# First differences taken by GpSimd between two normalizations' small steps, and the last tile's copy and difference in two halves

## The chip, the cores and the metric

The kernel runs on one core of one Trainium2 chip. The metric is the device time of one execution in microseconds (us). A core has TensorE (PE in the profile; its weight loads are listed as PEld), VectorE (DVE), ScalarE (ACT) and GpSimd (POOL), each with an instruction queue of its own that is worked off in order, and SyncE (SP), which issues the DMAs here. The engines are kept in step by semaphores: an instruction can wait for a semaphore to reach a value and can raise one when it is done.

## The reference

A Flamingo-style block over x of shape 4 x 2048 x 512, all in float32:

```python
x = x + tanh(g_xattn) * xattn(layernorm(x), ctx)      # 16 heads of 32, 154 context tokens, Wq Wk Wv Wo
x = x + tanh(g_ffn) * ffn(layernorm(x))

def ffn(x):                                           # x_prev: the token before, zero for the first
    xr = mu_r * x + (1 - mu_r) * x_prev
    xk = mu_k * x + (1 - mu_k) * x_prev
    r = sigmoid(xr @ W_r.T)
    k = xk @ W_k.T
    return r * (square(relu(k)) @ W_v.T)
```

Since mu * x + (1 - mu) * x_prev is mu * (x - x_prev) + x_prev, the kernel needs the difference of each token and the one before it. That difference is what the change is about.

## The kernel before

The 8192 tokens are worked in 16 blocks of N = 512 tokens; a block is TT = 4 tiles of 128 tokens, and the 512 channels are C = 4 chunks of 128. Each engine has a function step(i, ffn, pre), written out by hand: step 0 and step 15 stand alone and steps 1 to 14 are the body of a loop. The order of the instructions in each engine's step is the order of the work; nothing else schedules it. In step i the attention of block i, the feed-forward part of block i - 1 and the queries of block i + 1 are interleaved.

Matmuls in float32 are done as three products of a rounded high part and a low part. So a value that goes into a product is first mixed or copied (into a PSUM bank or a buffer), then ScalarE writes the high part (line 543), and VectorE or GpSimd subtracts it to get the low part (line 780 on VectorE, 463, 471 and 475 on GpSimd).

The stretch around the change is the second layernorm and the token mix. For block i, tile t:

- VectorE, residual (lines 879 to 884): x1 = projection + x (line 882), then the moments: bn_stats (811), the negated mean nm (814), bn_aggr (816).
- GpSimd, norm(1, i, t) (lines 434 to 445): three small operations on 128 x 1 values: variance plus epsilon (439), its power -1/2, rstd (441), and the bias nb (445). For t = 3 the third is left out.
- The normalized tile xn2: ScalarE for t = 0, 1, 2 (norm2, line 597), VectorE for t = 3 (norm2_last, line 890: a subtract and a multiply with one value per partition, SBUF to SBUF, 128 x 512).
- TensorE, x2_transposed (lines 1202 to 1211): four 128 x 128 transposes (line 1073) into o_bank or d_bank.
- ScalarE, x2_copy (lines 654 to 658): the bank is copied to x2, chunks by channels, tokens along the free dimension.
- The first difference diff = x2 - x2 shifted by one token, from SBUF to SBUF, 128 x 512 for a tile: GpSimd for t = 0, 1, 2 (difference, lines 452 to 459), VectorE for t = 3 (difference_last, lines 893 to 897). In the profile diff has the name place, since it lies in that tensor.
- VectorE, mix_k (lines 904 to 909): xk = diff * mu_k + x2 for a whole chunk (all 512 tokens), into o_bank or d_bank; both tensor inputs lie in SBUF. ScalarE then writes the high part of xk (xk_high), VectorE the low part (xk_low), and TensorE's ffn_k of the next step waits for xk_low chunk by chunk (line 1222).

GpSimd's order in this stretch is norm 0, norm 1, difference 0, norm 2, norm 3, difference 1, difference 2 (lines 518 to 524), and then it waits until all four chunks are mixed (line 526). VectorE's is residual 0 to 3 with maxima between, norm2_last, difference_last, mix_k 0 and 1, xk_low 0, gated (line 877, the feed-forward product of the block before), xk_low 1, mix_k 2 and 3, xk_low 2 and 3 (lines 1016 to 1036). TensorE's is the last projection, x2_transposed 1, query 3 of the next block with x2_transposed 2 before its last chunk, x2_transposed 3, ffn_v of tile 3 of the block before, maxima 4, and then the next step's ffn_k (lines 1353 to 1361).

Of the kernel before, what the change touches and what calls it, by code (L numbers as in the profile page):

```python
# [8 lines left out]
ALU = mybir.AluOpType  # L9
ACT = mybir.ActivationFunctionType  # L10
# [7 lines left out]
def flamingo_block(nc, x, ctx_columns, g_xattn, g_ffn, Wq, Wk, Wv, Wo, W_r, W_k, W_v, mu_r, mu_k, out):  # L18
# [8 lines left out]
    P = 128  # L27
    C = D // P
    G = H // 4
    N = 512  # L30
    TT = N // P
# [17 lines left out]
    with ExitStack() as ctx:  # L49
# [6 lines left out]
        def sem(name):  # L56
            return ctx.enter_context(nc.semaphore(name))
# [58 lines left out]
        diff = place[:, 4:8, :]  # L116
# [48 lines left out]
        x2_done, x2_ready = sem("x2_done"), sem("x2_ready")  # L165
        x2_first, carry_ready = sem("x2_first"), sem("carry_ready")
        diff_ready = sem("diff_ready")
        xn2_last, diff_last = sem("xn2_last"), sem("diff_last")
        xk_mixed, xk_hi = sem("xk_mixed"), sem("xk_hi")
        xr_mixed, xr_hi = sem("xr_mixed"), sem("xr_hi")  # L170
        xk_lo, xr_lo = sem("xk_lo"), sem("xr_lo")
# [12 lines left out]
        x2_bank = [(o_bank, d_bank)[t % 2] for t in range(TT)]  # L184
# [209 lines left out]
        def _(pool):  # L394
# [39 lines left out]
            def norm(which, i, t):  # L434

                n = i * TT + t + 1
                last = which == 1 and t == TT - 1
                pool.wait_ge(mean_ready[which], 2 * n)
                nc.gpsimd.tensor_tensor(ve[:, which, t:t + 1], mv[:, which, t, 1:2], eps[:, :], ALU.add).then_inc(var_eps_ready[which], 1)  # L439
                pool.wait_ge(var_eps_ready[which], n)  # L440
                nc.gpsimd.tensor_tensor(rstd[:, which, t:t + 1], ve[:, which, t:t + 1], minus_half[:, :], ALU.pow).then_inc(rstd_ready[which], 1)
                if last:
                    return
                pool.wait_ge(rstd_ready[which], n)
                nc.gpsimd.tensor_tensor(nb[:, which, t:t + 1], nm[:, which, t:t + 1], rstd[:, which, t:t + 1], ALU.mult).then_inc(norm_ready[which], 1)  # L445
# [6 lines left out]
            def difference(i, t):  # L452

                pool.wait_ge(x2_ready, i * TT + t + 1)
                if t == 0:
                    pool.wait_ge(x2_first, i + 1)
                    pool.wait_ge(attn_hi, (i + 1) * G)
                tokens, before = slice(1 + P * t, 1 + P * t + P), slice(P * t, P * t + P)
                nc.gpsimd.tensor_tensor(diff[:, :, before], x2[:, :, tokens], x2[:, :, before], ALU.subtract).then_inc(diff_ready, 1)
# [35 lines left out]
            def step(i, ffn, pre):  # L495
                if ffn:
                    k2_parts(i - 1)
                if pre:
                    norm(0, i + 1, 0)
                    norm(0, i + 1, 1)  # L500
                for g in range(1, G):
                    attn_low(i, g - 1)
                    if ffn:
                        output(i - 1, g - 1)
                    if pre:
                        for t in ((2, 3), (), ())[g - 1]:
                            norm(0, i + 1, t)
                attn_low(i, G - 1)
                if pre:
                    for g in range(G - 1):  # L510
                        q_low(i + 1, g)
                if not ffn:

                    pool.wait_ge(kv_done, KV_UNITS)
                    for n in range(7):
                        pool.wait_ge(later_stored[n], LATER_STORES[n])
                first_column(i)
                norm(1, i, 0)
                norm(1, i, 1)
                difference(i, 0)  # L520
                norm(1, i, 2)
                norm(1, i, 3)
                for t in range(1, TT - 1):
                    difference(i, t)

                pool.wait_ge(xk_mixed, (i + 1) * C)
                if pre:
                    q_low(i + 1, 3)
                if ffn:
                    output(i - 1, TT - 1)  # L530
# [10 lines left out]
        def _(act):  # L541
# [112 lines left out]
            def x2_copy(i, t):  # L654
                act.wait_ge(x2_done, i * TT + t + 1)
                later(act, r_done, i * TT)
                nc.scalar.activation(x2[:, :, 1 + P * t:1 + P * t + P],
                                     x2_bank[t][:, :].rearrange("p (c n) -> p c n", c=C), ACT.Copy).then_inc(x2_ready, 1)

            def mix_high(i, dst, c, src, mixed_ready, hi_ready):  # L660
                act.wait_ge(mixed_ready, i * C + c + 1)
# [116 lines left out]
        def _(dve):  # L778
# [111 lines left out]
                nc.vector.tensor_scalar(xn2[t % 2], x1[:, t, :], mv[:, 1, t, 0:1], rstd[:, 1, t:t + 1],  # L890
                                        ALU.subtract, ALU.mult).then_inc(xn2_last, 1)

            def difference_last(i):
                dve.wait_ge(diff_ready, (i + 1) * (TT - 1))
                dve.wait_ge(x2_ready, (i + 1) * TT)
                nc.vector.tensor_tensor(diff[:, :, N - P:N], x2[:, :, N - P + 1:N + 1], x2[:, :, N - P:N],
                                        ALU.subtract).then_inc(diff_last, 1)

            def keep_carry(i):
                dve.wait_ge(x2_ready, (i + 1) * TT)  # L900
# [1 line left out]
                nc.vector.tensor_copy(carry[:, :], x2[:, :, N]).then_inc(carry_ready, 1)  # L902

            def mix_k(i, c):
                if c == 0:
                    dve.wait_ge(diff_last, i + 1)
                elif c >= 2:
                    dve.wait_ge(xk_lo, i * C + c - 1)
                nc.vector.scalar_tensor_tensor(xk_bank[c][:, :], diff[:, c, :], mu[:, 1, c:c + 1], x2[:, c, 0:N], ALU.mult, ALU.add).then_inc(xk_mixed, 1)  # L909

# [42 lines left out]
            def step(i, ffn, pre):  # L953
                reduce_max(i, 4)
                if ffn:
                    mix_r(i - 1, 0)
                else:
                    kv_low_part(G + 1)
                reduce_max(i, 5)
                if not ffn:  # L960
                    ctx_low(1)
                if ffn:
                    xr_low(i - 1, 0)
                    mix_r(i - 1, 1)
                    mix_r(i - 1, 2)
                    xr_low(i - 1, 1)
                    mix_r(i - 1, 3)
                    xr_low(i - 1, 2)
                    k_relu(i - 1, 2)
                p_low(i, 0, 0)  # L970
                if ffn:
                    xr_low(i - 1, 3)
                p_low(i, 0, 1)
                p_low(i, 0, 2)
                p_low(i, 0, 3)
                if not ffn:
                    kv_low_part(FIRST_LATER)
                p_low(i, 0, 4)
                if ffn:
                    k_relu(i - 1, 3)  # L980
                if not ffn:
                    fill_group(0)
                if pre:
                    moments1(i + 1, 0)
                    moments1(i + 1, 1)
                for g in range(1, G):
                    attend(i, g - 1)
                    p_low(i, g, 0)
                    p_low(i, g, 1)
                    if ffn and g == 2:  # L990
                        gated(i - 1, 1, V_BANK[1])
                    if not ffn and g == 3:
                        kv_low_part(KV_UNITS - 1)
                    if pre and g == 3:
                        xT_low(i + 1, 0)
                    p_low(i, g, 2)
                    p_low(i, g, 3)
                    if not ffn and g < 3:
                        kv_low_part(FIRST_LATER + 2 * g)
                    p_low(i, g, 4)  # L1000
                    if ffn and g != 2:
                        gated(i - 1, g - 1, V_BANK[g - 1])
                    if not ffn and g < 3:
                        fill_group(g)
                    if pre and g == 1:
                        moments1(i + 1, 2)
                        moments1(i + 1, 3)
                if pre:
                    for t in range(1, TT):
                        xT_low(i + 1, t)  # L1010
                attend(i, G - 1)
                if pre:
                    reduce_max(i + 1, 0)
                    reduce_max(i + 1, 1)
                    reduce_max(i + 1, 2)
                residual(i, 0, pre)
                if pre:
                    reduce_max(i + 1, 3, (0, 1))
                residual(i, 1, pre)
                if pre:  # L1020
                    reduce_max(i + 1, 3, (2, 3))
                residual(i, 2, pre)
                residual(i, 3, pre)
                norm2_last(i)
                difference_last(i)
                mix_k(i, 0)
                mix_k(i, 1)
                xk_low(i, 0)
                if ffn:
                    gated(i - 1, TT - 1, V_BANK[TT - 1] if pre else V3_END)  # L1030
                xk_low(i, 1)
                mix_k(i, 2)
                mix_k(i, 3)
                xk_low(i, 2)
                xk_low(i, 3)
                keep_carry(i)
# [380 lines left out]
```

## Time and profile before

| | us |
|---|---|
| median of 3 runs | 1425.04 |
| the 3 runs | 1425.04, 1425.04, 1422.91 |
| the profiled execution: its time | 1423.38 |
| the profiled execution: its span | 1421.7 |
| PE busy in the span | 1355.7 (95%) |
| DVE busy | 1054.9 (74%) |
| ACT busy | 776.1 (55%) |
| POOL busy | 577.2 (41%) |
| mean granted TensorE clock | 0.989 of full speed |

The busy shares are of the span. A share of 95% for TensorE says that the time is its own work plus its pauses; a pause is what another engine can take away or add. The other engines are idle much of the time, so their work costs something only where TensorE, or the chain that TensorE waits for, has to wait for it.

### The profile page before, as it was taken

To read this page: it belongs to the slowest core of one execution; us is meant where nothing else is said; L and a number is where in the kernel's file an instruction comes from. 1 tells how busy PE (TensorE), PEld (TensorE's weight loads), DVE (VectorE), ACT (ScalarE), POOL (GpSimd) and SP (SyncE) were. 2 spreads that over 40 slices of the span, in tenths; PEclk is the share of its full clock that TensorE was granted. 3 is DMA by queue.
4 is the path that set the end of the run, shared out by engine and by line. 5 is a ranking of instruction groups with operands and counts; after the bars stand their busy time and mean duration, and the time that the engine had idled before them with its cause. 6 is when DMAs were issued, how large, how long until landed. Compare 5 with 4: busy or idle time off the path is not lost.

```text
span 1421.7 us, 27928 instructions
## 1 busy us (share of the span) xinstructions
PE 1355.7 (95%) x9436; PEld 990.4 (70%) x9436; DVE 1054.9 (74%) x1924; ACT 776.1 (55%) x1424; POOL 577.2 (41%) x774
## 2 busy tenths in 40 slices
PE   4989999999999999999999999999999999999988
PEld 3656676776767777676777767677776767777657
DVE  4887778687787868778686877868677786877652
ACT  3583746557374654737466473645637465563632
POOL 2113435344353534435253443525335352534333
PEclk7999999999999999999999999999999999999989
DMA  6631111211012121111212111121201112120101
GB/s 190 219 87 44 40 45 52 73 52 52 22 66 59 52 73 52 47 27 59 66 52 73 38 48 39 59 66 52 66 25 63 44 59 66 52 65 17 45 15 45
DMA packets 98795, 84.07 MB, mean 59 GB/s; under 512 B 49488, under 2 KB 63824, under 8 KB 98768
## 3 DMA queue, kind: packets, MB, share of 16 engines
q1 hardware_dynamic: 98768, 83.72, 19.5%
q8 instruction: 15, 0.25, 0.1%
q14 instruction: 12, 0.10, 0.0%
HBM read 58.79 MB, written 20.71 MB: 56 GB/s over the span
## 4 chain that ended last, share of the span: by engine, by line
PE 75%; DVE 13%; ACT 8%; issue 3%; POOL 1%; DMA 0%; ACTq 0%; DVEq 0%
PE g_bank L1067 41%; PE g_bank L1227 7%; PE o_bank L1174 6%; PE s_bank L1148 4%; PE d_bank L1180 4%; ACT s_bank L638 3%; ACT pq L637 3%; PE s_bank L1124 3%; PE s_bank L1158 2%; DVE buf L780 2%; DVE o_bank L909 2%; ACT buf L543 1%; DVE xa L890 1%; DVE d_bank L909 1%; PE s_bank L1067 1%
## 5 line engine op out<-in xcount | busy, mean ns | idle before, releaser
L850 DVE TENSOR_TENSOR pq<-s_bank,pq 128x512 f16<-128x512 f32 x320 | 220.2, 689 | 69.4 <-ACT s_bank L638 69.1
L846 DVE TENSOR_REDUCE mm<-s_bank 128x3 f32<-128x462 f32 (+1 forms) x384 | 198.8, 577 | 92.9 <-PE s_bank L1124 92.7
L637 ACT ACTIVATE pq<-s_bank 128x512 f16<-128x512 f32 x320 | 192.1, 600 | 86.6 <-PE s_bank L1152 86.6
L1227 PE MATMUL g_bank<-buf,WkT 128*128 128x512 f32 x744 | 196.6, 411 | 12.8 <-DVE buf L780 12.7
L1067 PE MATMUL g_bank<-xnT,WqT 128*128 128x512 f32 x768 | 199.2, 405 | 4.4 <-DVE xnT L834 4.4
L638 ACT ACTIVATE s_bank<-s_bank 128x512 f32<-128x512 f32 x320 | 194.6, 608 | 0.0
L1067 PE MATMUL g_bank<-WoT,buf 128*128 128x512 f32 x768 | 193.3, 401 | 0.0
L1067 PE MATMUL g_bank<-WrT,buf 128*128 128x512 f32 x744 | 184.2, 396 | 0.0
L475 POOL TENSOR_TENSOR buf<-place,buf 128x512 fp32r<-128x512 f32 x64 | 82.6, 1291 | 235.4 <-ACT buf L543 235.4
L1227 PEld LDWEIGHTS g_bank<-buf,WkT 128*128 128x128 f32 x744 | 136.6, 192 | 55.9 <-DVE buf L780 17.5
L1067 PE MATMUL g_bank<-WvT,buf 128*128 128x512 f32 x708 | 174.2, 395 | 0.0
L1067 PEld LDWEIGHTS g_bank<-xnT,WqT 128*128 128x128 f32 x768 | 139.7, 190 | 40.5 <-DVE xnT L834 5.9
L1067 PEld LDWEIGHTS g_bank<-WrT,buf 128*128 128x128 f32 x744 | 137.8, 188 | 40.2 <-issue 11.3
L1067 PEld LDWEIGHTS g_bank<-WoT,buf 128*128 128x128 f32 x768 | 140.7, 188 | 32.7
L1067 PEld LDWEIGHTS g_bank<-WvT,buf 128*128 128x128 f32 x708 | 130.6, 188 | 32.5 <-issue 5.8
L463 POOL TENSOR_TENSOR buf<-xa,buf 128x512 fp32r<-128x512 f32 x64 | 82.2, 1284 | 168.9 <-DVE d_bank L909 89.5
L543 ACT ACTIVATE buf<-place 128x512 fp32r<-128x512 f32 x128 | 81.0, 633 | 106.3 <-DVE place L867 71.7
L471 POOL TENSOR_TENSOR buf<-place,buf 128x512 fp32r<-128x512 f32 x64 | 83.3, 1301 | 93.9 <-ACT buf L543 93.9
L483 POOL TENSOR_TENSOR x<-place,x 128x512 f32<-128x512 f32 x48 | 61.7, 1285 | 123.1 <-DVE place L877 123.1
L597 ACT ACTIVATE xa<-x,nb,rstd 128x512 f32<-128x512 f32 x48 | 39.0, 812 | 105.3 <-POOL nb L445 104.9
L439 POOL TENSOR_TENSOR ve<-mv,eps 128x1 f32<-128x1 f32 x128 | 24.3, 190 | 164.2 <-DVE mv L816 164.2
L467 POOL TENSOR_TENSOR place<-place 128x512 f32<-128x512 f32 x64 | 78.0, 1218 | 25.5 <-ACT place L629 25.5
(140 smaller groups left out, 2096.4 us busy)
## 6 DMA issues: line engine op xcount, KB each, us to landing
xa<-in_x SPq DMA_DIRECT2D x64, 256.0 KB, 3.4
x<-in_x SPq DMA_DIRECT2D x64, 256.0 KB, 2.8
out<-x SPq DMA_DIRECT2D x48, 256.0 KB, 2.0
k_all<-k_scratch SPq DMA_DIRECT2D x16, 256.0 KB, 2.9
k_low<-k_scratch SPq DMA_DIRECT2D x16, 256.0 KB, 3.0
v_main<-v_scratch SPq DMA_DIRECT2D x16, 256.0 KB, 2.8
place<-x SPq DMA_DIRECT2D x16, 256.0 KB, 2.4
out<-place SPq DMA_DIRECT2D x16, 256.0 KB, 2.0
```

The source lines that it names most:

```text
L463: nc.gpsimd.tensor_tensor(buf4[:, LO, g, :], q32[g], buf4[:, HI, g, :].bitcast(F32), ALU.subtract).then_inc(q_lo, 1)
L467: nc.gpsimd.tensor_tensor(k2[c % 2], k2[c % 2], k2[c % 2], ALU.mult).then_inc(k2_ready, 1)
L471: nc.gpsimd.tensor_tensor(buf1[:, LO, c, :], k2[c % 2], buf1[:, HI, c, :].bitcast(F32), ALU.subtract).then_inc(k2_lo, 1)
L475: nc.gpsimd.tensor_tensor(buf3[:, LO, g, :], attn32, buf3[:, HI, g, :].bitcast(F32), ALU.subtract).then_inc(attn_lo, 1)
L543: nc.scalar.activation(dst, src, ACT.Copy).then_inc(done, 1)
L637: nc.scalar.activation(pq[:, n, HI, :], bank[:, :], ACT.Exp, scale=SCALE).then_inc(p_hi, 1)
L638: nc.scalar.activation(bank[:, :], bank[:, :], ACT.Exp, scale=SCALE).then_inc(p_full, 1)
L846: nc.vector.reduce_max(maxima, scores, AX.X).then_inc(reduced, 1)
L850: nc.vector.tensor_tensor(pq[:, n, LO, :], score_bank[5 * g + n][:, :], pq[:, n, HI, :], ALU.subtract).then_inc(p_lo, 1)
L1067: ins = nc.tensor.matmul(dst, stationary(s, c), moving(m, c), start=(c, n) == (0, 0), stop=(c, n) == (chunks - 1, len(PRODUCTS) - 1))
L1174: nc.tensor.matmul(o_bank[rows(j), :], v, pq[:, 4 if n else j, q, :], start=(n, k) == (0, 0), stop=(n, k) == (1, 2))
L1227: ins = nc.tensor.matmul(bank[c][:, :], WkT2[:, s, e, cols(c)], buf3[:, m, e, :], start=(e, n) == (0, 0), stop=(e, n) == (C - 1, len(PRODU ...
```

## The change

Three things are changed.

1. GpSimd's order: difference 1 now stands between norm 2 and norm 3, and difference 2 after norm 3. Nothing is added or taken away on GpSimd.
2. The copy of the last tile (x2_copy with t = 3, ScalarE) is two instructions of two chunks each. The first raises the new semaphore x2_half, the second raises x2_ready.
3. difference_last (VectorE) is two instructions of two chunks each, each with its own semaphore. mix_k 0 stands between them and waits only for the first; mix_k 2 waits for the second.

```diff
@@ gpsimd step
                 difference(i, 0)
                 norm(1, i, 2)
+                difference(i, 1)
                 norm(1, i, 3)
-                for t in range(1, TT - 1):
-                    difference(i, t)
+                difference(i, 2)
@@ scalar
             def x2_copy(i, t):
                 act.wait_ge(x2_done, i * TT + t + 1)
                 later(act, r_done, i * TT)
-                nc.scalar.activation(x2[:, :, 1 + P * t:1 + P * t + P],
-                                     x2_bank[t][:, :].rearrange("p (c n) -> p c n", c=C), ACT.Copy).then_inc(x2_ready, 1)
+                dst, src = x2[:, :, 1 + P * t:1 + P * t + P], x2_bank[t][:, :].rearrange("p (c n) -> p c n", c=C)
+                if t < TT - 1:
+                    nc.scalar.activation(dst, src, ACT.Copy).then_inc(x2_ready, 1)
+                else:
+                    nc.scalar.activation(dst[:, 0:2, :], src[:, 0:2, :], ACT.Copy).then_inc(x2_half, 1)
+                    nc.scalar.activation(dst[:, 2:4, :], src[:, 2:4, :], ACT.Copy).then_inc(x2_ready, 1)
@@ vector
-            def difference_last(i):
-                dve.wait_ge(diff_ready, (i + 1) * (TT - 1))
-                dve.wait_ge(x2_ready, (i + 1) * TT)
-                nc.vector.tensor_tensor(diff[:, :, N - P:N], x2[:, :, N - P + 1:N + 1], x2[:, :, N - P:N],
-                                        ALU.subtract).then_inc(diff_last, 1)
+            def difference_last(i, half):
+                if half == 0:
+                    dve.wait_ge(diff_ready, (i + 1) * (TT - 1))
+                    dve.wait_ge(x2_half, i + 1)
+                else:
+                    dve.wait_ge(x2_ready, (i + 1) * TT)
+                chunks = slice(2 * half, 2 * half + 2)
+                nc.vector.tensor_tensor(diff[:, chunks, N - P:N], x2[:, chunks, N - P + 1:N + 1], x2[:, chunks, N - P:N],
+                                        ALU.subtract).then_inc(diff_last[half], 1)
             def mix_k(i, c):
-                if c == 0:
-                    dve.wait_ge(diff_last, i + 1)
-                elif c >= 2:
+                if c % 2 == 0:
+                    dve.wait_ge(diff_last[c // 2], i + 1)
+                if c >= 2:
                     dve.wait_ge(xk_lo, i * C + c - 1)
@@ vector step
-                difference_last(i)
+                difference_last(i, 0)
                 mix_k(i, 0)
+                difference_last(i, 1)
                 mix_k(i, 1)
```

## Rows read from the trace of the kernel before

**Rows 1.** Windows: one loop body; length, PE busy (instructions), granted clock, DMA, GB/s.

```profile
631.90:715.60 83.70, 82.19 (x583) 1.00 0.17 53
```

**Rows 2.** Timeline of TensorE, steady stretch: start, duration, engine, line, idle before and releaser.

```profile
655.75 0.83 PE L1174 MATMUL o_bank<-pq,v_main 128*32 128x512 f16 x12 [0.49 <-DVE pq L850]
...
715.50 0.95 PE L1067 MATMUL g_bank<-xnT,WqT 128*128 128x512 f32 x3
716.90 0.66 PE L1073 MATMUL d_bank<-ident,xa 128*128 128x128 f32 x4 [0.45 <-DVE xa L890]
...
721.19 3.05 PE L1227 MATMUL g_bank<-buf,WkT 128*128 128x512 f32 x12 [0.40 <-DVE buf L780]
724.41 3.06 PE L1227 MATMUL g_bank<-buf,WkT 128*128 128x512 f32 x12 [0.17 <-DVE buf L780]
```

**Rows 3.** Timeline of VectorE over the same stretch.

```profile
715.59 1.25 DVE L890 TENSOR_SCALAR xa<-x,mv,rstd 128x512 f32<-128x512 f32 x1 [0.94 <-POOL rstd L441]
718.30 0.69 DVE L896 TENSOR_TENSOR place<-x 128x512 f32<-128x512 f32 x1 [1.45 <-ACT x L657]
719.02 0.76 DVE L909 SCALAR_TENSOR_TENSOR o_bank<-place,mu,x 128x512 f32<-128x512 f32 x1
719.69 0.76 DVE L909 SCALAR_TENSOR_TENSOR d_bank<-place,mu,x 128x512 f32<-128x512 f32 x1
720.45 0.69 DVE L780 TENSOR_TENSOR buf<-o_bank,buf 128x512 fp32r<-128x512 f32 x1
```

**Rows 4.** Timeline of GpSimd over the same stretch.

```profile
710.71 1.04 POOL L459 TENSOR_TENSOR place<-x 128x512 f32<-128x512 f32 x1
...
714.73 0.19 POOL L439 TENSOR_TENSOR ve<-mv,eps 128x1 f32<-128x1 f32 x1 [1.39 <-DVE mv L816]
715.00 0.55 POOL L441 TENSOR_TENSOR rstd<-ve,minus_half 128x1 f32<-128x1 f32 x1
715.52 2.22 POOL L459 TENSOR_TENSOR place<-x 128x512 f32<-128x512 f32 x2
```

**Rows 5.** Timeline of ScalarE: the four copies to x2 lie at line 657.

```profile
710.03 0.60 ACT L657 ACTIVATE x<-o_bank 128x512 f32<-128x512 f32 x1 [1.66 <-PE o_bank L1073]
...
713.26 0.60 ACT L657 ACTIVATE x<-d_bank 128x512 f32<-128x512 f32 x1 [1.79 <-PE d_bank L1073]
...
715.78 0.60 ACT L657 ACTIVATE x<-o_bank 128x512 f32<-128x512 f32 x1 [1.22 <-PE o_bank L1073]
717.59 0.60 ACT L657 ACTIVATE x<-d_bank 128x512 f32<-128x512 f32 x1 [1.21 <-PE d_bank L1073]
718.09 0.59 ACT L543 ACTIVATE buf<-g_bank 128x512 fp32r<-128x512 f32 x1
```

**Rows 6.** Lines 890 (all 16), 783, 459 (two here): duration ns min/median/max.

```profile
L890 DVE TENSOR_SCALAR xa<-x,mv,rstd x16: 1254/1254/1255, 128.5 to 1376.4; 128x512 f32<-128x512 f32 x16
...
L783 DVE CAST negsel<-place x1: 427/427/427, 3.2 to 3.2; 128x512 fp32r<-128x512 f32 x1
...
L459 POOL TENSOR_TENSOR place<-x x2: 1040/1131/1222, 715.5 to 716.5; 128x512 f32<-128x512 f32 x2
```

**Rows 7.** Timeline of VectorE and GpSimd where they lie side by side elsewhere.

```profile
740.36 1.04 POOL L467 TENSOR_TENSOR place<-place 128x512 f32<-128x512 f32 x1
...
740.46 0.22 DVE L814 TENSOR_SCALAR nm<-stats 128x1 f32<-128x1 f32 x1
...
1318.12 0.76 DVE L919 SCALAR_TENSOR_TENSOR d_bank<-place,mu,x 128x512 f32<-128x512 f32 x1
...
1318.26 1.51 POOL L467 TENSOR_TENSOR place<-place 128x512 f32<-128x512 f32 x1
```

**Rows 8.** Groups of instructions by shape, first 110 us: halves of 128x256; mean ns last.

```profile
L780 DVE TENSOR_TENSOR buf<-s_bank,buf 128x256 fp32r<-128x256 f32 x4 | 1.7, 424 | 8.7 <-ACT buf L543 8.7
L543 ACT ACTIVATE buf<-s_bank 128x256 fp32r<-128x256 f32 x4 | 1.5, 368 | 2.3 <-PE s_bank L1067 2.3
```

**Rows 9.** Timeline of TensorE in the last step.

```profile
1377.73 0.66 PE L1073 MATMUL d_bank<-ident,xa 128*128 128x128 f32 x4 [0.94 <-DVE xa L890]
```

More of the change, by code:

```diff
@@ L167, in flamingo_block @@
         diff_ready = sem("diff_ready")
-        xn2_last, diff_last = sem("xn2_last"), sem("diff_last")
+        xn2_last, x2_half = sem("xn2_last"), sem("x2_half")
+        diff_last = [sem("diff_last01"), sem("diff_last23")]
         xk_mixed, xk_hi = sem("xk_mixed"), sem("xk_hi")
```

## The prediction

> **What bounds the kernel now.** I read the windows first, to see how far TensorE fills a loop body; then TensorE's timeline for its pauses; then the chain of waits to see what each pause hangs on; then the timelines of the other engines around it. A loop body takes 83.70 us, of which TensorE is busy 82.19 at full clock [rows 1]. The 1.51 us of pause stand at four places [rows 2]: 0.49 before an attention product (here from the body before; it comes back once per body), 0.45 before the last tile's transposes at 716.90, 0.40 before ffn_k at 721.19, and 0.17 before its third chunk at 724.41. The last three hang on one chain, which a reader can follow through the rows: GpSimd's rstd of tile 3 ends at 715.55 [rows 4], norm2_last runs 715.59 to 716.84 [rows 3], the transposes start at 716.90, ScalarE copies them 717.59 to 718.19 [rows 5], then difference_last at 718.30, mix_k 0 at 719.02, mix_k 1 at 719.69, xk_low 0 from 720.45 to 721.14 [rows 3], and TensorE at 721.19. From there VectorE goes on without a break to xk_low 2, for which TensorE waits at 724.41. So a microsecond off this chain is a microsecond per body, as long as TensorE is not the later one.
>
> **Norm2_last, and what stands beside it.** It takes 1254 ns in each of its 16 instances, while the only other one-input 128x512 operation of VectorE from SBUF to SBUF with no partner on GpSimd took 427 [rows 6]. Difference 1 of GpSimd starts at 715.52, 0.07 us before norm2_last, and is the 1040 ns one of the two in that row, so it ends at 716.56; norm2_last ends 0.28 later. Difference 2, queued behind it, takes 1222 in place of 1040 [rows 4, 6]. That is how two instructions look that cannot run together: VectorE's waits for difference 1 to end, and difference 2 then waits for VectorE's. Once VectorE is first with two SBUF inputs, GpSimd's operation lasts 1.51 us instead of 1.04 [rows 7].
>
> The Trainium skill, page "SBUF — State Buffer", section "Who interferes with whom", states this as a rule: a VectorE tensor_scalar in a two-port mode and a GpSimd instruction exclude each other, and the second one blocks until the first is done. By that rule norm2_last costs its free duration once difference 1 is out of its way; without it the 1254 ns would be its own and stay. The trace agrees with the rule, by the 1254, the 427 and the stretched 1222.
>
> **Part 1, GpSimd's order.** Difference 1 now needs x2_copy 1, which ends at 713.86; a copy's end is followed by the difference 0.08 later where GpSimd is free (710.63, then 710.71) [rows 4, 5]. So it runs 713.94 to 714.98. The next GpSimd instruction starts 1.00 after it (the two differences of 1.04 and 1.22 fill 2.22, the second starting at 716.52), at 714.94, where norm 3 started at 714.73: norm 3 is 0.21 late. This is the cost of the move. It is queued on rstd: rstd ends 715.76, norm2_last starts 715.80. VectorE's operations beside difference 1 are residual 3, bn_stats, nm and bn_aggr. Difference 0 lies beside the same of tile 2 and takes 1.04; for the 128x1 operation there is a row of its own, 0.22 us inside a GpSimd operation of 1.04 [rows 7], so I charge nothing. If nm were held till 714.98, it would cost 0.6 in norm 3 (bound, below).
> Norm2_last without a partner: 427 by its nearest row, 280 if only what was left after difference 1 counts, 1254 if it is its own. I take 430: it ends 716.23, 0.61 earlier than 716.84. Difference 2 waits for x2_copy 2 (ends 716.38 [rows 5]) and starts 716.46, after norm2_last, and ends 717.50. TensorE has its last query matmuls from 715.50 for 0.95, the successors in such a queue start about 0.15 before that modelled end, at 716.30; so the transposes start at about 716.29 instead of 716.90. TensorE is just free: its 0.45 pause goes. ScalarE's copy starts 716.98 instead of 717.59; its copy 2 is over by then.
>
> **Parts 2 and 3, the halves.** A half costs ScalarE 368 ns and VectorE 424 [rows 8], against 600 and 692 for the whole, so two halves cost about 140 and 160 ns more. ScalarE: first half 716.98 to 717.35, second from 717.25 (whole ones overlap by 0.10 [rows 5]) to 717.62. The query copies behind them start 0.03 after that minus overlap, still 0.5 earlier than before: hidden. VectorE: by x2_half difference_last could start at 717.46 (0.11 after its release, as 718.19 to 718.30), but it also waits for difference 2, which ends at 717.50; with the second wait behind it I take 717.60. Difference 2 is the new last release here. Then 0.45 to mix_k 0 (718.05), 0.67 to the second half (718.72; 0.67 is the distance of the two mixes [rows 3]), 0.45 to mix_k 1 (719.17), 0.67 to xk_low 0 (719.84), whose high part is long there. Before it was 720.45, since xk_low 0 had to wait for the high part of chunk 0. Gain: 0.61. With one whole difference it would be 717.67, mix_k 0 at 718.39, high part done at 719.78, xk_low 0 at 719.82: the halves give nothing and cost nothing, -0.02 to +0.02. The range for the halves: 0.13 better if difference 2 is not what is waited for, 0.13 worse if a half costs VectorE 0.49 in place of 0.42.
>
> The Trainium skill, "VectorE: DVE Perf Modes", section "The TRN2 errata", speaks against halves: a fixed cost per instruction, which many small tiles pay each. The rows agree (2 x 424 against 692), and that cost is in the sum.
>
> **Behind it.** Gated follows at 720.44; it needs ffn_v 3, which TensorE starts at 716.70 instead of 717.31 and ends at 719.7. ffn_k starts at 720.58 instead of 721.19, its third chunk at 723.80 instead of 724.41, because VectorE's queue from xk_low 0 on has the same instructions at the same distances. The fourth pause (0.49, waiting for attention weights that ScalarE and VectorE made from scores that TensorE made) starts from TensorE's own instructions and shifts with it. GpSimd waits after difference 2 for all four mixes, so nothing is queued there; SyncE's copy of x1 starts on norm2_last, earlier too.
>
> **Sum.** 15 steps (0 to 14) x 0.61 = 9.15. The last step has another TensorE order: the transposes wait 0.94 for norm2_last [rows 9], and ffn_k waits for xk_low 0 alone. With norm2_last at 1376.42 + 0.21 + 0.43 = 1377.06 and difference 2 no longer late, the same steps give 0.7. Together 9.85, or 9.9 us: 1423.4 of the profiled execution becomes 1413.5. The runs shown are 1422.91 to 1425.04 with the median at the upper end, so the median of the changed kernel lies between 1413.0 and 1415.2; I say 1414.5.
>
> **Rivals.**
> - *Nm is held by difference 1.* nm 714.98, rstd ends 716.15, norm2_last 716.19 to 716.62, difference 2 starts after it and ends 717.7, difference_last 717.8: a gain of 0.41 per step, 6.6 us, 1418. For it: nm is a tensor_scalar like norm2_last. Against: the 0.22 us one of [rows 7]. The same time comes out if difference 2 or the halves cost 0.2 more than I take. Chance 0.17.
> - *The later pause takes it back.* If the 0.49 pause hangs on something that does not shift (a load, GpSimd's queue), it grows to up to 1.1 and the gain is near 0: 1422 to 1426. For it: nothing in the rows but that this is the pause that I follow least. Against: its releaser is VectorE behind ScalarE behind TensorE. Chance 0.08.
> - *Slower: norm2_last is long by itself, and the move only delays it.* Then it starts 0.21 late and still takes 1254. Transposes at 717.11, first half copied at 718.18, difference_last 718.29, xk_low 0 at 720.53: 0.08 per step, 1.3 us, which is no change. It gets slower from the point where difference 1 in front of norm 3 takes 1222 rather than 1040: 0.39 late, 0.26 per step, 4.2 us, 1429. For it: 1254 never varies. Against: the 427 and the 280 left. Chance 0.05.
> - Otherwise my forecast, 0.55 to 0.75 per step, 1411.5 to 1416.5 with the spread of runs: 0.70.
>
> Two medians of this kernel can be told apart from about 0.2%, 2.85 us. Faster by more than that: forecast and first rival, 0.87. Within: second rival, 0.08. Slower: 0.05. The range takes in the forecast and the first rival: 1411.5 to 1419.5.
>
> **What would show it.** Right: line 890's operation at about 430 ns and 0.2 later behind bn_aggr; difference 1 before norm 3's three rows at 1040 ns; both later differences at 1040; TensorE's pause before the last transposes gone, those before ffn_k (0.4 and 0.17) and the 0.49 nearly as they were; difference_last's first half released by GpSimd's difference 2; a body of 83.1 us. Wrong: norm2_last still at 1254; nm stretched beside difference 1; the pause before ffn_k grown by what the transposes gained; a body of 83.5 or more.

## The result and the profile after

| | before | after |
|---|---|---|
| median, us | 1424.68 (4 runs, 1422.91 to 1425.04) | 1410.05 (4 runs, 1407.83 to 1411.68) |
| ratio, 95% interval | | 0.9898 [0.9882, 0.9914] |
| profiled execution, us | 1423.38 | 1411.68 |
| its span, us | 1421.7 | 1409.9 |
| all runs of this study, us | mean 1423.8 (44), median 1424.2 | mean 1411.3 (21, 1407.8 to 1414.6), median 1410.5 |

The changed kernel is 14.6 us faster by the first medians. That is below the forecast (1414.5) and 1.5 us below its range (1411.5 to 1419.5). Over all runs the gain of the means is 12.5 us (1423.8 to 1411.3). The forecast was 9.9.

First the windows of the changed kernel (same columns as [rows 1]): two loop bodies.

```profile
630.30:713.24 82.94, 82.14 (x581) 1.00 0.18 54
713.24:796.18 82.94, 82.14 (x581) 1.00 0.17 54
```

A body went from 83.70 to 82.94 us, 0.76 us less, which makes 11.4 us in 15 steps. TensorE's busy time hardly moved (82.19 to 82.14), so 0.71 of the 0.76 are pause: 1.51 us per body before, 0.80 after. Next the timeline of VectorE in the second of these bodies, the answer to [rows 3].

```profile
713.24 0.55 DVE L898 TENSOR_SCALAR xa<-x,mv,rstd 128x512 f32<-128x512 f32 x1 [1.14 <-POOL rstd L443]
715.02 0.43 DVE L908 TENSOR_TENSOR place<-x 128x256 f32<-128x256 f32 x1 [1.24 <-POOL place L461]
715.48 0.76 DVE L921 SCALAR_TENSOR_TENSOR o_bank<-place,mu,x 128x512 f32<-128x512 f32 x1
716.15 0.42 DVE L908 TENSOR_TENSOR place<-x 128x256 f32<-128x256 f32 x1
716.48 0.75 DVE L921 SCALAR_TENSOR_TENSOR d_bank<-place,mu,x 128x512 f32<-128x512 f32 x1
717.15 0.69 DVE L788 TENSOR_TENSOR buf<-o_bank,buf 128x512 fp32r<-128x512 f32 x1
```

Norm2_last (line 898 now) takes 546 ns instead of 1254. The first half of the difference is released by GpSimd's difference 2, which ends at 714.94. ScalarE's first half of the copy, which it also needs, ends 0.02 earlier:

```profile
714.53 0.39 ACT L665 ACTIVATE x<-d_bank 128x256 f32<-128x256 f32 x1 [0.70 <-PE d_bank L1086]
```

The second half of the difference starts at 716.15 and mix_k 1 only 0.33 behind it; the prediction had put 0.45 there. GpSimd's timeline, to set beside [rows 4]:

```profile
711.38 1.04 POOL L461 TENSOR_TENSOR place<-x 128x512 f32<-128x512 f32 x1 [0.59 <-ACT x L662]
712.38 0.19 POOL L441 TENSOR_TENSOR ve<-mv,eps 128x1 f32<-128x1 f32 x1
712.65 0.55 POOL L443 TENSOR_TENSOR rstd<-ve,minus_half 128x1 f32<-128x1 f32 x1
713.90 1.04 POOL L461 TENSOR_TENSOR place<-x 128x512 f32<-128x512 f32 x1 [0.70 <-ACT x L662]
```

Difference 1 stands ahead of norm 3, and no difference lies beside norm2_last (713.24 to 713.79) any more; differences 1 and 2 take 1.04 each. Difference 2 starts 0.08 behind the copy of its tile (713.22 to 713.82 on ScalarE), for which it waits. TensorE's timeline, to set beside [rows 2]:

```profile
712.94 0.95 PE L1080 MATMUL g_bank<-xnT,WqT 128*128 128x512 f32 x3
713.84 0.66 PE L1086 MATMUL d_bank<-ident,xa 128*128 128x128 f32 x4
...
717.89 3.07 PE L1240 MATMUL g_bank<-buf,WkT 128*128 128x512 f32 x12
721.11 3.05 PE L1240 MATMUL g_bank<-buf,WkT 128*128 128x512 f32 x12 [0.16 <-DVE buf L788]
...
736.16 0.83 PE L1187 MATMUL o_bank<-pq,v_main 128*32 128x512 f16 x12 [0.49 <-DVE pq L858]
```

The pause before the transposes (0.45) is gone. The one before ffn_k went from 0.40 to 0.15 (the work before it ends at 717.74), so short that its row no longer lists it. The 0.17 (now 0.16) and the 0.49 stand as they were: 0.15, 0.16 and 0.49 are the 0.80 that are left. So the gain was carried through the whole body, and nothing further on took it back.

### The profile page after: what moved, and what is told of

Its sections match the earlier page's. It is cut to its first block, busy times and chain, and to the rows that moved or that the text cites. A ratio compares the mean times of both kernels' runs of the same rounds, so it can differ in the third digit from the quotient of the medians.

```text
span 1409.9 us, 27976 instructions
## 1 busy us (share of the span) xinstructions
PE 1357.0 (96%) x9436; PEld 991.6 (70%) x9436; DVE 1043.5 (74%) x1940; ACT 777.4 (55%) x1440; POOL 574.7 (41%) x774
## 4 chain that ended last, share of the span: by engine, by line
PE 79%; DVE 9%; ACT 8%; issue 3%; POOL 0%; DMA 0%; ACTq 0%; DVEq 0%
PE g_bank L1080 45%; PE g_bank L1240 7%; PE o_bank L1187 6%; PE s_bank L1161 4%; PE d_bank L1193 4%; ACT s_bank L641 3%; ACT pq L640 3%; PE s_bank L1137 3%; PE s_bank L1171 2%; DVE buf L788 2%; PE d_bank L1086 2%; DVE o_bank L921 2%; PE o_bank L1086 1%; DVE d_bank L921 1%; ACT buf L546 1%
## 5 line engine op out<-in xcount | busy, mean ns | idle before, releaser
L469 POOL TENSOR_TENSOR place<-place 128x512 f32<-128x512 f32 x64 | 78.2, 1222 | 24.4 <-ACT place L632 24.4
L869 DVE STREAM_TRANSPOSE place<-d_bank 128x512 f32<-128x512 f32 x64 | 45.4, 709 | 55.5 <-PE d_bank L1193 55.5
```

The costliest lines, as they stand in the source:

```text
L469: nc.gpsimd.tensor_tensor(k2[c % 2], k2[c % 2], k2[c % 2], ALU.mult).then_inc(k2_ready, 1)
```

## The experiments

The body of a kernel is measured here as the distance of line 890's instruction (or the one that stands for it) over seven bodies in the middle of the trace, divided by seven. In four traces of the changed kernel it came out between 82.93 and 82.99.

### Which part brings what: order_only and halves_only

order_only is the kernel before with this edit:

```diff
                 norm(1, i, 2)
+                difference(i, 1)
                 norm(1, i, 3)
-                for t in range(1, TT - 1):
-                    difference(i, t)
+                difference(i, 2)
```

> Only GpSimd's order is changed; copy and difference of the last tile stay whole. Theory A (norm2_last stood behind difference 1, and the halves give the rest): norm2_last 546 ns as in the changed kernel, difference 2 at 1040; copy 3 ends 0.50 us earlier than before, difference_last starts 0.51 earlier, xk_low 0 starts 0.52 earlier, since it now waits for the high part of chunk 0. Body 83.18 us, 8 us off in all. Theory B (as predicted: the halves are worth nothing, -0.02 to +0.02): body as in the changed kernel, 82.94, and 11 to 12 us off.

Measured: 1416.12 us (5 runs, 1415.69 to 1418.38) beside 1423.56, ratio 0.9954 [0.9941, 0.9967]; body 83.20. VectorE's timeline of order_only:

```profile
716.46 0.55 DVE L891 TENSOR_SCALAR xa<-x,mv,rstd 128x512 f32<-128x512 f32 x1 [1.15 <-POOL rstd L441]
718.46 0.69 DVE L897 TENSOR_TENSOR place<-x 128x512 f32<-128x512 f32 x1 [1.45 <-ACT x L658]
719.19 0.76 DVE L910 SCALAR_TENSOR_TENSOR o_bank<-place,mu,x 128x512 f32<-128x512 f32 x1
719.85 0.76 DVE L910 SCALAR_TENSOR_TENSOR d_bank<-place,mu,x 128x512 f32<-128x512 f32 x1
720.61 0.69 DVE L781 TENSOR_TENSOR buf<-o_bank,buf 128x512 fp32r<-128x512 f32 x1
```

From norm2_last's start to xk_low 0's: 4.15 us, against 4.86 before [rows 3]. That is 0.71 less, of which 0.21 go for the late start: 0.50 per body. TensorE's pause of 0.45 before the transposes is gone, and the one before ffn_k is still 0.38. Theory A holds, and order alone is not the whole change. The difference is released here by ScalarE's copy, which hangs on norm2_last, so here norm2_last's own length counts in full.

halves_only is the changed kernel with the reverse of that edit, so GpSimd's order is as before.

> GpSimd's order as before, copy and difference of the last tile in halves. Theory A: norm2_last is back at 1254 ns and TensorE's pause of 0.45 before the last transposes is back; difference_last's first half starts at the same offset less 0.21, mix_k 1 follows its half at 0.33, xk_low 0 is 0.25 earlier than before: body 83.45 us, 3.5 to 4 us off. Theory B (halves worth nothing): body 83.70, time as before.

Measured: 1419.18 us (8 runs, 1417.04 to 1420.84) beside 1423.56, ratio 0.997 [0.996, 0.998]; body 83.48. VectorE and TensorE in the timeline of halves_only:

```profile
713.81 1.25 DVE L897 TENSOR_SCALAR xa<-x,mv,rstd 128x512 f32<-128x512 f32 x1 [0.94 <-POOL rstd L443]
718.43 0.68 DVE L787 TENSOR_TENSOR buf<-o_bank,buf 128x512 fp32r<-128x512 f32 x1
...
715.12 0.66 PE L1085 MATMUL d_bank<-ident,xa 128*128 128x128 f32 x4 [0.45 <-DVE xa L897]
719.17 3.06 PE L1239 MATMUL g_bank<-buf,WkT 128*128 128x512 f32 x12 [0.16 <-DVE buf L787]
```

Norm2_last is at 1254 ns again, TensorE waits 0.45 for it, and xk_low 0 starts 4.62 after norm2_last instead of 4.86, which makes 0.24. Of these, 0.21 come from the copy: its first half is done earlier, and the difference starts 2.50 behind norm2_last's start instead of 2.71. TensorE's pause before ffn_k falls from 0.40 to 0.16. So the two parts act on two different pauses: the order on the one before the transposes, the halves on the one before ffn_k. The halves are worth 0.22 us per body by themselves and 0.21 to 0.27 on top of the order (83.20 to between 82.93 and 82.99). The parts add up: 0.50 and 0.22 against 0.71 to 0.77 together. The prediction gave the halves nothing; that was wrong.

### The term that was mis-sized: mix1_waits

```diff
             def mix_k(i, c):
-                if c % 2 == 0:
-                    dve.wait_ge(diff_last[c // 2], i + 1)
+                if c <= 2:
+                    dve.wait_ge(diff_last[(c + 1) // 2], i + 1)
```

> The changed kernel with one wait more: mix_k 1 also waits for the second half of difference_last, which it does not need. This is the timeline that the prediction worked out. If the missing 0.12 to 0.15 us per step of the forecast is this wait, the distance from the second half to mix_k 1 becomes 0.45 instead of 0.33, the body goes from 82.94 to 83.06 or 83.08, and the time is 1.5 to 2.2 us above the changed kernel. If the forecast was off for another reason, the body stays at 82.94.

Body 83.10. VectorE's timeline of mix1_waits:

```profile
712.82 0.42 DVE L908 TENSOR_TENSOR place<-x 128x256 f32<-128x256 f32 x1 [1.24 <-POOL place L461]
713.28 0.76 DVE L921 SCALAR_TENSOR_TENSOR o_bank<-place,mu,x 128x512 f32<-128x512 f32 x1
713.94 0.42 DVE L908 TENSOR_TENSOR place<-x 128x256 f32<-128x256 f32 x1
714.40 0.76 DVE L921 SCALAR_TENSOR_TENSOR d_bank<-place,mu,x 128x512 f32<-128x512 f32 x1
715.07 0.68 DVE L788 TENSOR_TENSOR buf<-o_bank,buf 128x512 fp32r<-128x512 f32 x1
```

From the second half to mix_k 1: 0.46 (713.94 to 714.40) instead of 0.33. From the first half to xk_low 0: 2.25 instead of 2.13, and so in every body looked at. TensorE's pause before ffn_k is 0.27 (0.15 without the wait). The forecast had 2.24 and a gain of 0.61 per body; this kernel gains 0.60. So the timeline that was predicted is that of this kernel, which has one wait more than the change.

Its median, 1411.77 (5 runs, 1409.64 to 1412.91), lies 2.0 below that of the changed kernel in the same comparison (1413.78, next section), where 2 us above was expected. The medians do not show what the body shows; the reason is next.

### What the body does not explain: after_again, after_third, after_fourth

These are the changed kernel, unaltered.

> The changed kernel unaltered, for more times beside the kernel before and for a second trace. If what the body does not explain (14.6 us of medians against 12.1 from 15 bodies of 0.76 and a last step of 0.73) is chance in where TensorE's granted clock falls to half, the body is again 82.94, the difference of medians comes nearer to 12 to 13 us, and the trace has its half-clock stretches at other places than the first one or another number of them. If it is part of the change, the difference stays at 14 or more and the last step's stretches are again one instead of three.

> The changed kernel again, beside the version with the half on GpSimd and for the spread of its times. Body 82.94 again. If the half-clock stretches are chance, its span less half of the time at the lower clock is again 1394 us (1409.9 - 15.9 and 1412.1 - 18.2 so far), wherever they lie.

> The changed kernel beside it. Body 82.94 to 83.00; single times anywhere from 1408 to 1414, median near 1411.

| | median, us (runs) | span of the trace | body | half-clock time | span less half of it |
|---|---|---|---|---|---|
| before | 1424.68 (4) | 1421.7 | 83.70 | 31.4 | 1406.0 |
| after | 1410.05 (4) | 1409.9 | 82.93 | 31.6 | 1394.1 |
| after_again | 1413.78 (6) | 1412.1 | 82.96 | 34.2 | 1395.0 |
| after_third | 1409.98 (5) | 1408.2 | 82.99 | 24.4 | 1396.0 |
| after_fourth | 1409.22 (6) | 1407.7 | 82.96 | 28.0 | 1393.7 |
| mix1_waits | 1411.77 (5) | 1407.9 | 83.10 | 22.5 | 1396.7 |

Half-clock time is 2 x (1 - granted clock) x length, summed over windows of 5 us up to the end of the span: at clock 0.5 a window counts whole. (The expectations above counted some time behind the end of the span too; the table does not.) Besides one stretch of 14 to 17 us that starts near 20 us in each of these traces, stretches of 3.4 us (6.8 where two lie together) at half clock come in the first 140 us and the last 80, and their places differ between executions of one program. Here are two places, in the windows of after and then of after_third.

```profile
55.00:65.00 10.00, 8.28 (x50) 0.83 0.67 203
100.00:110.00 10.00, 9.32 (x66) 0.83 0.41 85
```

```profile
55.00:65.00 10.00, 7.21 (x48) 1.00 0.69 219
100.00:110.00 10.00, 9.71 (x83) 1.00 0.49 104
```

Between 100 and 110 us TensorE started 83 matmuls at full clock and only 66 with a stretch. What one costs can be read where two traces of the changed kernel part. Up to 1346 us after_again runs 1.9 us behind after_fourth. Then comes its stretch at 1347, and from 1356 on it is 3.5 behind, so that stretch cost 1.6 us. Between 55 and 65 us, where TensorE also has pauses, a stretch did not lower the number of matmuls (50, and 48 at full clock).

The traces of the changed kernel differ by 4.4 us in span and by 2.3 in the last column, where the expectation had 1394 for each. So only part of the spread between them follows these stretches. The mean granted clock of each single run is on record as well (to 0.001, which is 1.4 us). Taking (1 - clock) x span off each span brings the standard deviation of the changed kernel's 21 runs from 2.2 to 0.9 us, so most of the spread of its times goes with the clock. mix1_waits had the least half-clock time, which hides its loss of 2 us. With the clock taken out its mean is 1396.2 (5 runs) against 1394.4 for after_again (6 runs): 1.8 above, as expected.

All runs together (44 of before, 21 of after) give 12.5 us between means, with standard errors of 0.2 and 0.5; 15 bodies of 0.76 and a last step of 0.73 give 12.1. (Last step: from the end of projection 3 to ffn_k 8.48 us before, 7.75 after.) With the mean of the four traces' bodies, 82.96, it is 11.8. With each run's clock taken out as above, the means are 1406.0 (the 40 runs of before that have a clock) and 1394.6 (21), 11.4 apart; the other 1.0 us is that before lost 16.0 us to the lower clock and the changed kernel 15.0. Whether that 1.0 is chance or belongs to the change is not shown. The 14.6 of the first four runs were 2 us of luck.

Why a stretch comes where it does is open. TensorE makes the same pause of 2.5 us in after_again (it ends at 1346.0), before (1355.1) and after_third (1344.7). In the first two a stretch at half clock begins about 1 us behind it, in the third none.

### Is it the collision: short_diff1

```diff
+                if t == 1:
+                    tokens, before = slice(1 + P * t, 2 + P * t), slice(P * t, P * t + 1)
                 nc.gpsimd.tensor_tensor(diff[:, :, before], ...)
```

> The kernel before, its order untouched, with difference 1 on GpSimd cut to one token (the other 127 of that tile are left out of the difference). Theory A (norm2_last's 1254 ns are the wait for difference 1): norm2_last 546 ns at its old start, xk_low 0 about 0.7 earlier, body 83.0. Theory B (1254 ns are its own): norm2_last stays at 1254 and the body at 83.70.

Measured: 1412.5 us (4 runs, 1412.39 to 1413.75) beside 1424.12, ratio 0.9926 [0.9911, 0.9941]; body 83.04. GpSimd and VectorE in the timeline of short_diff1:

```profile
710.64 0.55 POOL L441 TENSOR_TENSOR rstd<-ve,minus_half 128x1 f32<-128x1 f32 x1
711.16 0.20 POOL L461 TENSOR_TENSOR place<-x 128x4 f32<-128x4 f32 x1
...
711.23 0.55 DVE L892 TENSOR_SCALAR xa<-x,mv,rstd 128x512 f32<-128x512 f32 x1 [0.94 <-POOL rstd L441]
```

Same order, same start 0.94 after bn_aggr, and norm2_last takes 548 ns as soon as the difference in front of it is short. So 0.71 of the 1254 ns were a wait for GpSimd's instruction. How exactly norm2_last waited is not shown: in [rows 3] and [rows 4] only 0.28 us of it lie behind the end of difference 1, less than the 0.55 that it takes alone. The gain is 0.66 per body, near the 0.70 expected.

### Is freeing norm2_last enough: diff_behind_norm

```diff
                 norm(1, i, 3)
+                pool.wait_ge(xn2_last, i + 1)
                 for t in range(1, TT - 1):
                     difference(i, t)
```

> The kernel before, in which GpSimd waits for norm2_last before difference 1. Norm2_last is then free and not late: 546 ns. Theory A (both ends count: norm2_last, and difference 2, for which difference_last waits): difference 1 runs 1.04 from the end of norm2_last, difference 2 ends 2.1 after it, difference_last starts 0.05 later than in the kernel before though its copy is done 0.7 earlier; body 83.70 to 83.80, no gain. Theory B (only norm2_last counts, and any way to free it is as good): body 83.0, 10 us off.

Measured: 1423.71 us (10 runs, 1422.54 to 1425.59) beside 1424.12, ratio 1.0002 [0.9992, 1.0011]; body 83.75. The timeline of diff_behind_norm, GpSimd, then VectorE, then TensorE:

```profile
716.45 2.05 POOL L459 TENSOR_TENSOR place<-x 128x512 f32<-128x512 f32 x2 [0.66 <-DVE xa L891]
...
715.83 0.55 DVE L891 TENSOR_SCALAR xa<-x,mv,rstd 128x512 f32<-128x512 f32 x1 [0.94 <-POOL rstd L441]
718.53 0.69 DVE L897 TENSOR_TENSOR place<-x 128x512 f32<-128x512 f32 x1 [2.16 <-POOL place L459]
...
721.43 3.05 PE L1228 MATMUL g_bank<-buf,WkT 128*128 128x512 f32 x12 [1.03 <-DVE buf L781]
```

Norm2_last is free (0.55) and early, the transposes are early too, and all of it is lost again: difference_last now waits 2.16 us for difference 2, and TensorE's pause before ffn_k grows from 0.40 to 1.03. Difference 1 has to be off norm2_last's time and still be early. That is what the place between norm 2 and norm 3 does, for 0.21 us.

### A version that goes on: half_on_gpsimd

VectorE's queue up to xk_low 2 is what TensorE's last pause in the stretch (0.16) hangs on. GpSimd stands idle for 5.5 us there. In the edit below (shortened at the dots), mix_k 1 waits for x2_ready, which the removed call had done for it.

```diff
@@ gpsimd step
                 difference(i, 2)
+                pool.wait_ge(x2_ready, (i + 1) * TT)
+                pool.wait_ge(xk_mixed, i * C + 2)
+                nc.gpsimd.tensor_tensor(diff[:, 2:4, N - P:N], ...).then_inc(diff_last[1], 1)
@@ vector step
                 mix_k(i, 0)
-                difference_last(i, 1)
+                dve.wait_ge(x2_ready, (i + 1) * TT)
                 mix_k(i, 1)
```

> The changed kernel with the second half of the last tile's difference moved from VectorE to GpSimd, which waits for mix_k 1 first, so that it lies beside xk_low 0 and gated (one SBUF input and one from PSUM) and ahead of mix_k 2. Theory A (VectorE's queue up to xk_low 2 is what TensorE waits for last): 0.33 us leave that queue, but xk_low 0 then waits for its high part and xk_low 2 likewise; xk_low 2 starts 0.25 earlier, TensorE's third chunk too; body 82.69 against 82.94, 3.5 to 4 us below the changed kernel. Theory B (TensorE is the later one by now, or GpSimd's half meets a mix and holds it up by its 0.55 us): body 82.94 or above, no gain or up to 8 us lost.

> The version with the half on GpSimd again, since its median of 4 times lay only 0.3 us below the changed kernel's of 5, while its body is 82.74 against 82.93 to 83.00. If the body decides and half-clock stretches (3.4 us each, of which up to 1.7 us are lost) only blur it, then over both calls its median is 3 to 4 us below the changed kernel's, and its span less half of its half-clock time is near 1390 again (1409.3 - 19.2). If the move has a cost outside the loop body, the medians stay equal.

Body 82.74 and 82.71 in two traces. Medians 1409.68 (4 runs, 1406.43 to 1411.06), ratio to before 0.9896 [0.9881, 0.9911], and 1409.53 (5 runs, 1404.14 to 1410.39), ratio 0.9888 [0.9872, 0.9905]. The timeline of half_on_gpsimd, GpSimd and TensorE:

```profile
715.71 0.61 POOL L530 TENSOR_TENSOR place<-x 128x256 f32<-128x256 f32 x1 [2.10 <-DVE d_bank L925]
...
716.35 5.32 PE L1244 MATMUL g_bank<-buf,WkT 128*128 128x512 f32 x20
```

The half lies where it meets no mix, and TensorE runs through ffn_k without a pause; only the 0.49 further on is left of the four. Theory A holds by the body: 0.25 us less than the trace of the changed kernel taken beside each (82.99 to 82.74, 82.96 to 82.71), as expected. In time, the mean of its 9 runs is 1408.7, that of the 21 of the changed kernel 1411.3: 2.5 us, with standard errors of 0.7 and 0.5. Side by side the medians were only 0.3 us apart, once this way and once the other, where 3 to 4 us were expected, so the times alone leave it unclear. The granted clock settles it: the spans of its traces less half their half-clock time are 1390.5 and 1390.9 (near 1390 was expected), and the same over all 9 runs, by each run's clock, is 1390.9 against 1394.6. That is 3.7 us less, about what 15 bodies of 0.25 make.

## Why the prediction was wrong

The mechanism held, and the gain was larger than forecast. By its steps:

- *The collision.* Right. Norm2_last was held for difference 1 (short_diff1). Free it takes 546 ns, not the 430 taken from the cast. For the changed kernel that cost nothing, since difference_last's first half waits for difference 2, as predicted; but the forecast had 0.15 us to spare there, and 0.02 were left. In the forecast's comparison with one whole difference it did cost, see below.
- *Norm 3 is 0.21 late.* Right: it starts 1.00 after difference 1 began, norm2_last's idle time went from 0.94 to 1.14, and its nm and bn_aggr beside difference 1 keep 0.21 and 0.17 us.
- *Difference 2 becomes the last release of difference_last.* Right; it is named as releaser in the row at 715.02.
- *"0.45 to mix_k 1".* Wrong, and this is the step that failed. The distance of an instruction that waits for the one before it was put on a pair that has no such wait: mix_k 1 needs chunk 1, which lies in the first half, so it starts 0.33 behind the second half. That is 0.13 us per body, 2 us in all: the forecast would have been about 12 us, as against 11.8 to 12.1 by the bodies and the last step. mix1_waits puts the wait in and gives the predicted timeline.
- *"The halves give nothing and cost nothing".* Wrong: they bring 0.21 to 0.27 us per body. About half of that is the same step. The other half is norm2_last's 430 ns: with one whole difference the copy, and so norm2_last, is what is waited for. The forecast had xk_low 0 there 4.02 after norm2_last's start (715.80 to 719.82), order_only has 4.15. With the halves it had 4.04, and the changed kernel has 3.91. The two errors of 0.13, less the 0.02 that the forecast put between the two versions, are the 0.24 between 4.15 and 3.91.
- *Everything behind shifts.* Right: the pauses of 0.17 and 0.49 stayed. That the 0.40 before ffn_k would stay "nearly" as it was did not fit the forecast's own 0.61, of which only 0.45 are the pause before the transposes; it became 0.15, and 0.27 in mix1_waits.
- *The last step.* Right: 0.7 was forecast, 0.73 measured.
- *The range.* It took the three runs of before (2.1 us apart) for the spread and had no room above the forecast's own band. The changed kernel's runs lie 6.7 us apart, mostly with the half-clock stretches at start and end. With 12.1 us in place of 9.9 the forecast would have stood at about 1412.3, inside the range. So of the 4.4 us between the forecast (1414.5) and the first median (1410.05) about half is the mis-sized term, and the other half is the spread of the runs, for which a range that ends at 1411.5 had no room: the mean of all 21 runs is 1411.3 and their median 1410.5.

None of the rivals came: nm is not held, the later pause took nothing back, and norm2_last is not long by itself.

## What to carry to other kernels

An instruction whose duration never varies but is twice that of its like is worth a look at what the neighbouring engine does at that instant: it may be a wait that the profile books as work. When a queue is re-timed by hand, read off for each pair whether there is a wait between them; with a wait the successor starts a little after the end of the one before, without one 0.09 us ahead of it, and the difference was a sixth of this gain. And when a blocking instruction is moved, its own reader has a time too: behind norm2_last it cost all that it freed.

## What the runs showed of the hardware

- One semaphore wait of VectorE on its own instruction just before costs 0.13 us at this size: 0.46 against 0.33 between the starts of a 128x256 difference and the next mix.
- VectorE's subtract and multiply with two values per partition, 128x512 float32 from SBUF to SBUF, takes 546 ns when no GpSimd difference lies beside it and 1254 when one of 1040 ns has started 0.07 us earlier; the cast of the same size takes 427 [rows 6].
- VectorE's nm, the same kind of instruction on 128x1 values, takes 0.21 us beside difference 1 as it does elsewhere: it is not held.
- Executions of one program differ in the number and place of stretches of 3.4 us at half TensorE clock. One such stretch cost 1.6 us where TensorE had work. Single times of the changed kernel lie 6.7 us apart, most of it with the clock (standard deviation 2.2 us, 0.9 with the clock taken out), while the loop body repeats to 0.06 us; so for a change worth under 3 us the body of a trace said more than the median of five runs.
